# Linear attention and a squared-ReLU block on one core: values spread over the key features by broadcast DMAs instead of TensorE, normalised keys in a PSUM bank

## The reference, cut to what matters

```python
B, L, D, H, dk = 8, 512, 256, 16, 16
x = x + layernorm(attn(layernorm(x)))
x = x + layernorm(ffn(layernorm(x)))
# attn: q, k, v = x @ W_qkv.T, per head; k is normalised over its 16 features
def step(F, (q_t, k_t, v_t)):                 # scan over the 512 positions
    hebbian = einsum('bhd,bhe->bhde', v_t, k_t)
    F = retention * F + coef * hebbian        # retention, coef: [H, dk, dk]
    return F, einsum('bhde,bhe->bhd', W_LTM + F, q_t)
# y @ W_o.T follows
# ffn: y = square(relu(x @ W_fc.T)) @ W_proj.T, then a five-step spike count of y
```

## Time and profile before

| | before |
|---|---|
| median of 3 runs | 743.29 us (738.89 to 744.5) |
| profiled execution, own time | 738.58 us |
| its span | 736.8 us |
| TensorE busy | 605.3 us (82%) |
| VectorE busy | 544.8 us (74%) |
| GpSimd busy | 406.5 us (55%) |
| ScalarE busy | 338.1 us (46%) |
| DMA queue of SP | 20.02 MB, 7.8% of 16 engines |

### The profile page before, as it was taken

How to read it: one execution, slowest core, us unless ns; L and a number is a source line. 1 busy time by engine, 2 the same in 40 slices (tenths; PEclk the granted TensorE clock), 3 DMA queues, 4 the chain that set the end, 5 groups by cost and what they waited for, 6 DMA issues and landing times.

```text
span 736.8 us, 8225 instructions
## 1 busy us (share of the span) xinstructions
PE 605.3 (82%) x2760; PEld 407.2 (55%) x2768; DVE 544.8 (74%) x892; ACT 338.1 (46%) x631; POOL 406.5 (55%) x198
## 2 busy tenths in 40 slices
PE   0567778778999699988998899969998899778782
PEld 0343334435776477755775577647765576457471
DVE  4479999987898689977996789968996789722101
ACT  1422212333546644564446454664456433565644
POOL 0246775676468465865577546845586556631111
PEclk9969999899999999999999799999999999999897
DMA  7000100020000020002000110002000200020010
GB/s 262 28 0 1 57 1 0 1 85 1 0 1 30 0 87 1 29 1 87 0 30 1 50 37 1 28 2 85 1 1 1 86 1 0 1 85 1 0 58 28
DMA packets 16585, 21.58 MB, mean 29 GB/s; under 512 B 1184, under 2 KB 14880, under 8 KB 16416
## 3 DMA queue, kind: packets, MB, share of 16 engines
q1 hardware_dynamic: 16400, 20.02, 7.8%
q0 software_dynamic: 144, 1.05, 0.4%
HBM read 12.68 MB, written 4.19 MB: 23 GB/s over the span
## 4 chain that ended last, share of the span: by engine, by line
PE 54%; DVE 19%; issue 13%; ACT 8%; POOL 2%; DMA 2%; SPq 0%; POOLq 0%; ACTq 0%; DVEq 0%
PE p_c L358 10%; PE p_c L331 9%; DVE state L639 8%; PE p_a L253 8%; PE p_y L306 7%; PE p_rep L292 6%; DVE p_rep L630 5%; PE p_rep L293 5%; PE p_c L319 4%; ACT sign L510 3%; PE p_y L301 2%; DVE stats L595 2%; PE p_c L340 1%; POOL prod L757 1%; ACT x1f L445 1%
## 5 line engine op out<-in xcount | busy, mean ns | idle before, releaser
L757 POOL TENSOR_TENSOR prod<-state,qf 128x1024 f32<-128x1024 f32 x128 | 304.8, 2383 | 190.1 <-DVE state L639 188.0
L639 DVE TENSOR_TENSOR_SCAN state<-ret,p_rep 128x512 f32<-128x512 f32 x256 | 297.2, 1202 | 0.0
L630 DVE TENSOR_TENSOR p_rep<-p_rep,kf 128x1024 f32<-128x1024 f32 x128 | 156.4, 1222 | 75.4 <-PE p_rep L293 75.3
L292 PE MATMUL p_rep<-vh,pick_sb 128*128 128x512 f32 x256 | 118.2, 462 | 54.6 <-DVE state L639 48.3
L331 PE MATMUL p_c<-wproj_sb,ht 128*128 128x256 f32 x512 | 119.6, 383 | 1.3 <-ACT ht L500 1.3
L331 PEld LDWEIGHTS p_c<-wproj_sb,ht 128*128 128x128 f32 x512 | 95.1, 190 | 29.5 <-issue 15.1
L293 PE MATMUL p_rep<-vl,pick_sb 128*128 128x512 f32 x256 | 103.6, 405 | 0.0
L358 PE MATMUL p_c<-x1t,wfc_s 128*128 128x512 f32 x384 | 99.6, 404 | 3.3 <-ACT hr L498 3.3
L292 PEld LDWEIGHTS p_rep<-vh,pick_sb 128*128 128x128 f32 x256 | 50.0, 195 | 87.3 <-DVE state L639 70.0
L253 PE MATMUL p_a<-xt,wqkv_s 128*128 128x512 f32 x288 | 92.7, 464 | 4.6 <-issue 2.8
L358 PEld LDWEIGHTS p_c<-x1t,wfc_s 128*128 128x128 f32 x384 | 73.0, 194 | 23.2 <-issue 6.9
(11 more groups left out here) (92 smaller groups left out, 573.8 us busy)
## 6 DMA issues: line engine op xcount, KB each, us to landing
xa<-in_x SPq DMA_DIRECT2D x8, 512.0 KB, 3.5
x<-in_x SPq DMA_DIRECT2D x8, 512.0 KB, 3.4
x1k<-x SPq DMA_DIRECT2D x8, 512.0 KB, 2.9
out<-x1k SPq DMA_DIRECT2D x8, 512.0 KB, 2.8
pick_sb<-in_pick POOLq DMA_DIRECT2D x1, 1024.0 KB, 6.6
prod<-in_w_fc SPq DMA_DIRECT2D x1, 1024.0 KB, 8.0
wproj_sb<-in_w_proj SPq DMA_DIRECT2D x1, 1024.0 KB, 10.3
state<-in_w_qkv SPq DMA_DIRECT2D x1, 768.0 KB, 7.2
```

The lines of the kernel that those rows point to most:

```text
L292: pe.matmul(p_rep[s % 2][:, i, :], pick_sb[:, d, :], vh[:, half, :], start=True, stop=False)
L630: v.tensor_tensor(p_rep[s % 2][:, :, :], p_rep[s % 2][:, :, :], key, ALU.mult).then_inc(S["hebb_done"], 1)
L639: v.tensor_tensor_scan(state[:, s % NS, i, :], ret[:, r:r + 1].broadcast_to([P, L]), p_rep[s % 2][:, i, :], 0.0, ALU.mult, ALU.add).then_i ...
L757: p.tensor_tensor(prod[:, s % NZ, :, :], state[:, s % NS, :, :], qf[:, s // HS, :].unsqueeze(1).broadcast_to([P, 2, L]), ALU.mult).then_in ...
```

## The change

The four matmuls of a slot are gone, with `pick_sb`, `vh`, `vl`, the rounding on ScalarE and `low_v` on GpSimd. In their place, for each of the two features of a slot, the SP queue issues one DMA inside SBUF: the source is the 8 rows of `vf` that hold the feature (8 partitions x 512 values, 16 KB), each read 16 times, and the destination is one of 8 buffers `vrep` of 128x512 (256 KB). VectorE's product is cut into two instructions of 128x512; each reads `vrep` in SBUF and the normalised key `p_k`, which now lies in a PSUM bank, and writes one of three PSUM banks `p_u`. A buffer of `vrep` is filled again when the product 8 features earlier is done. The value projection now comes first of the three, so that the values are ready earlier, and turning the next input is a slot later. The key's normalisation of the second half moves from slot 6 to the start of slot 8, since there is one `p_k` for both halves. The copy `x1k` is gone: `x1` has two buffers in turn, and `store_out` and `load_again` stand between the broadcasts on the SP queue. The diff, cut (the same swap of order is made on ScalarE and in the prologue; semaphore names follow):

```diff
+NV = 8
+NU = 3
-        pick_sb = sb("pick_sb", [P, DK, P], F32R)
-        kf = sb("kf", [P, HALVES, L])
-        vf = sb("vf", [P, L])
-        vh = sb("vh", [P, HALVES, L], F32R)
-        vl = sb("vl", [P, HALVES, L], F32R)
+        vf = sb("vf", [P, HALVES, L])
+        vrep = sb("vrep", [P, NV, L])
-        x1 = sb("x1", [P, TILES, D])
-        x1k = sb("x1k", [P, TILES, D])
+        x1 = [sb(f"x1_{i}", [P, TILES, D]) for i in range(2)]
-        p_rep = [ps(f"p_rep{i}", [P, 2, L]) for i in range(2)]
+        p_u = [ps(f"p_u{i}", [P, L]) for i in range(NU)]
+        p_k = ps("p_k", [P, L])
...
+        v_in = [sem(f"v_in{i}") for i in range(NV)]
...
+            def spread_v(b, s):
+                half, features = step_features(s)
+                if s % HS == 0:
+                    sp.wait_ge(S["v_done"], 2 * b + half + 1)
+                for i, d in enumerate(features):
+                    n = 2 * (SLOTS * b + s) + i
+                    sp.wait_ge(S["hebb_done"], at(n - NV + 1))
+                    rows = vf[d * HH:(d + 1) * HH, half, :]
+                    sp.dma_start(vrep[:, n % NV, :], rows.unsqueeze(1).broadcast_to([HH, DK, L])).then_inc(
+                        v_in[n % NV], 16)
...
             load_x(1)
...
+            for g in range(B):
+                for s in range(SLOTS):
+                    spread_v(g, s)
+                    if s == 5 and g >= 3: store_out(g - 3)
+                    if s == 8 and g >= 1: load_again(g - 1)
+                    if s == 15 and g < B - 2: load_x(g + 2)
+            store_out(B - 3)
+            load_again(B - 1)
+            store_out(B - 2)
+            store_out(B - 1)
...
-            def replicate(b, s):
-                half, features = step_features(s)
-                if s % HS == 0:
-                    pe.wait_ge(S["v_low"], at(2 * b + half + 1))
-                for i, d in enumerate(features):
-                    pe.wait_ge(S["state_done"], at(2 * (SLOTS * b + s - 2) + i + 1))
-                    pe.matmul(p_rep[s % 2][:, i, :], pick_sb[:, d, :], vh[:, half, :], start=True, stop=False)
-                    last = pe.matmul(p_rep[s % 2][:, i, :], pick_sb[:, d, :], vl[:, half, :], start=False, stop=True)
-                last.then_inc(S["rep_done"], 1)
...
-                        if s == 0: project_k(g, 1)
-                        if s == 1: key_variance(g, 1)
-                        if s == 2: project_v(g, 1)
+                        if s == 0: project_v(g, 1)
+                        if s == 1: project_k(g, 1)
+                        if s == 2: key_variance(g, 1)
...
             def copy_v(b, half):
-                act.wait_ge(S["v_low"], at(2 * b + half))
-                copy(p_a[:, :], vf[:, :], "v_proj", 2 * b + half + 1, "v_done")
-                copy(vf[:, :], vh[:, half, :], "v_done", 2 * b + half + 1, "v_high")
+                act.wait_ge(S["hebb_done"], at(DK * (2 * (b - 1) + half + 1)))
+                copy(p_a[:, :], vf[:, half, :], "v_proj", 2 * b + half + 1, "v_done")
...
-                v.tensor_tensor(kf[:, half, :], p_a[:, :], kc[:, :], ALU.mult).then_inc(S["k_done"], 1)
...
+                dve.wait_ge(S["hebb_done"], DK * (2 * b + half))
+                v.tensor_tensor(p_k[:, :], p_a[:, :], kc[:, :], ALU.mult).then_inc(S["k_done"], 1)
+
+            def hebbian(b, s, i):
+                n = 2 * (SLOTS * b + s) + i
+                dve.wait_ge(v_in[n % NV], 16 * (n // NV + 1))
+                dve.wait_ge(S["state_done"], at(n - NU + 1))
+                if s % HS == 0 and i == 0:
                     dve.wait_ge(S["k_done"], at(2 * b + s // HS + 1))
-                key = kf[:, s // HS, :].unsqueeze(1).broadcast_to([P, 2, L])
-                v.tensor_tensor(p_rep[s % 2][:, :, :], p_rep[s % 2][:, :, :], key, ALU.mult).then_inc(
+                v.tensor_tensor(p_u[n % NU][:, :], vrep[:, n % NV, :], p_k[:, :], ALU.mult).then_inc(
                     S["hebb_done"], 1)
...
-                                     p_rep[s % 2][:, i, :], 0.0, ALU.mult, ALU.add).then_inc(S["state_done"], 1)
+                                     p_u[n % NU][:, :], 0.0, ALU.mult, ALU.add).then_inc(S["state_done"], 1)
...
+                    if now and s == HS: norm_k(g, 1)
...
-                    if now and s == 6: norm_k(g, 1)
...
-            def low_v(b, half):
-                rest(vf[:, :], vh[:, half, :], vl[:, half, :], "v_high", 2 * b + half + 1, "v_low")
-
-            p.dma_start(pick_sb[:, :, :], pick).then_inc(S["pick_in"], 16)
```

More of the change, by code:

```diff
@@ L210, in load_x @@
                 sp.dma_start(xa[:, :, :], by_tile(x, b)).then_inc(S["x_in"], 16)
[L212 to L223, removed]
@@ L225, in _ @@
-            load_x(1)
[L226 to L233, removed]
+            def spread_v(b, s):
[8 more added lines that the diff above has]
+                        v_in[n % NV], 16)
@@ new lines, in store_out, with load_again @@
+            def store_out(b):
+                sp.wait_ge(S["res_done"], at(b + 1))
+                sp.dma_start(by_tile(out, b), x1[b % 2][:, :, :]).then_inc(S["out_done"], 16)
+            def load_again(b):
+                sp.wait_ge(S["out_done"], at(16 * (b - 1)))
+                sp.dma_start(x1[b % 2][:, :, :], by_tile(x, b)).then_inc(S["again_in"], 16)
+            load_x(1)
+            for g in range(B):
[4 more added lines that the diff above has]
+                    if s == 15 and g < B - 2: load_x(g + 2)
@@ L416, in iteration @@
                             up(b1, 2)
-                    if after and s == SLOTS - 1: replicate(b, 0)
             run(iteration)
@@ L535, in iteration @@
                 for s in range(SLOTS):
-                    if now and s == 0: square_k(g, 1)
+                    if now and s == 0: copy_v(g, 1)
                     if two_before and s == 0: hidden(b2, 3)
                     if two_before and s == 1: hidden(b2, 4)
-                    if now and s == 1: key_deviation(g, 1)
+                    if now and s == 1: square_k(g, 1)
                     if two_before and s == 1: hidden(b2, 5)
-                    if now and s == 2: copy_v(g, 1)
+                    if now and s == 2: key_deviation(g, 1)
                     if before and s == 3: copy_y(b1, 1)
@@ L554, in iteration @@
                     if two_before and s == 13: signs(b2, 1)
-                    if after and s in (7, 8): copy_xt(b, s - 7)
+                    if after and s in (8, 9): copy_xt(b, s - 8)
                     if before and s == 10: deviation(3, b1)
-                    if after and s == 10: square_k(b, 0)
+                    if after and s == 10: copy_v(b, 0)
                     if now and s == 11: copy_y(g, 0)
-                    if after and s == 11: key_deviation(b, 0)
-                    if before and s == 11: norm(3, b1, x1, oo, "x1_done", b1 + 1)
+                    if after and s == 11: square_k(b, 0)
+                    if before and s == 11: norm(3, b1, x1[b1 % 2], oo, "x1_done", b1 + 1)
                     if before and s == 12:
@@ L563, in iteration @@
                         copy_x1t(b1, 1)
-                    if after and s == 12: copy_v(b, 0)
+                    if after and s == 12: key_deviation(b, 0)
                     if after and s == 13: copy_q(b, 0)
@@ L727, in iteration @@
                 for s in range(SLOTS):
-                    ends = (g, s - 1) if s > 0 else (b1, SLOTS - 1)
-                    if now: hebbian(g, s)
-                    if now if s > 0 else before: scan(*ends, 1)
-                    if now: scan(g, s, 0)
+                    if now and s == HS: norm_k(g, 1)
+                    first = s % HS == 0
+                    if now and not first: hebbian(g, s, 0)
+                    if s > 0 and now: scan(g, s - 1, 1)
+                    if s == 0 and before: scan(b1, SLOTS - 1, 1)
+                    if now:
+                        if first: hebbian(g, s, 0)
+                        hebbian(g, s, 1)
+                        scan(g, s, 0)
                     if after and s == 2: statistics(1, b, xa, "x_in", 16 * (b + 1))
@@ L735, in iteration @@
                     if before and s == 6: statistics(2, b1, oo, "o_done", 2 * (b1 + 1))
-                    if now and s == 6: norm_k(g, 1)
                     if before and s == 7: scales(2, b1)
-                    if before and s == 10: statistics(3, b1, x1, "x1_done", b1 + 1)
+                    if before and s == 10: statistics(3, b1, x1[b1 % 2], "x1_done", b1 + 1)
                     if before and s == 11: scales(3, b1)
@@ L796, in iteration @@
                     if s == 0 and before: read(b1, SLOTS - 1)
-                    if now and s == 4: low_v(g, 1)
                     if before and s == 8: add_attention(b1)
-                    if after and s in (8, 9): low_x(b, s - 8)
+                    if after and s in (9, 10): low_x(b, s - 9)
                     if before and s == 13:
@@ L802, in iteration @@
                         low_x1(b1, 1)
```

(1 more changed line is left out.)

51 lines of the change are left out of this document (21 added, 30 removed).

## The result

The changed kernel takes 1168.91 us (median of 4 runs, 1160.28 to 1171.25), the kernel before 742.1 in the same set. The ratio is 1.573, 95% interval 1.563 to 1.584: slower by 57%. The forecast was 1410 us with a range of 900 to 1600.

The account below looks back on a forecast made before the run. The prediction took the one DMA queue's broadcasts, bound by their few source partitions, to set the pace: 31.6 + 1262 + 23 + 0.6 + 94.8 = 1412 us of span, plus 1.8 outside it, 1414, rounded to 1410; range 900 to 1600.

Parts of the forecast that it names:

- The bound before, and what the change takes off: TensorE sets the pace at 81.3 us per iteration; losing 64 matmuls at 0.23 us takes off 14.7 us per iteration.
- The products: On VectorE, 32 products at 0.658 us replace 16 at 1224 ns: +1.5 us, 67.2 us busy per iteration.
- Start, whole-tile transfers, end: Outside the broadcasts: stream starts at 31.6 us, 18 whole-tile transfers take 23 us, last product to end takes 94.8 us.
- The broadcast, the deciding term: DMA queue: 256 broadcasts at 4.93 us each, 1262 us; an iteration cannot be shorter than 32 of them.
- c: Stream time of one 256 KB broadcast on the DMA queue; forecast 4.93 us, floor 0.62 to 1.23, ceiling 9.85.
- in between: Rival, chance 0.14: source gives more than twice a stream's rate, 2.3 to 4.4 us per broadcast; 997 us at 3.3.
- The likeliest case: Chance 0.66: DMA stream bound by its source, 4.4 to 5.7 us per broadcast, kernel 1280 to 1610 us.
- The doubling of a row's 26.6 GB/s: Broadcast source: twice the 26.6 GB/s of 8 partitions in the copy `x1k`, taken as 53.2 GB/s, 4.93 us per broadcast.
- The hidden rival: Rival, chance 0.17: broadcasts at most 1.23 us each are hidden, VectorE sets about 70 us per iteration, kernel 655 us.
- What the profile was to show: Signs: VectorE waiting for DMA over half the span, landing near eight times c, 67 MB more at some 50 GB/s.

## Why the prediction was right, and by how much

- **The bound before, and what the change takes off.** The 64 spreading matmuls of an iteration are gone. TensorE's pace no longer counts, as said: in the stretch from 300 to 500 us it is busy 109 of 200.
- **The products.** 0.658 us expected; 0.676 where they follow one another, 0.696 where VectorE had idled. VectorE's busy time in an iteration is 66.0 us with rows four apart, against 67.2.
- **Start, whole-tile transfers, end.** The first broadcast was issued at 29.9 (30.5 expected), and from the last product's start to the end it is 1168.1 - 1072.3 = 95.8 us (94.8).
- **The broadcast, the deciding term.** This is the step that was mis-sized: c = 4.93 us expected, 3.98 measured, 0.95 x 256 = 243 us, all of the difference between 1410 and 1169. The source's rate for one block, 53.2 GB/s as an estimate, was good: 51 measured with a fixed block. What failed is the sentence that blocks are read one after the other and that the eight buffers do not lift this. Overlap does lift it, where the next block is on another port: 2.97 us when every change of block allows it, 3.98 when every second does. By the Trainium skill (SBUF — State Buffer, Door 1: The DMA port swizzle) c would have been 4.82 us; for one block 5.10 was measured.
- **The case it fell in.** 3.98 us lies in the rival "in between" (2.3 to 4.4 us, chance 0.14), whose words were that streams share less evenly and blocks overlap; the overlap is what the runs show. The likeliest case (0.66) was 1280 to 1610 and did not come. The mechanism, a stream bound by its few source partitions, was right. The doubling of a row's 26.6 GB/s that priced one block had no row behind it; that it came out at 51 is luck as far as the rows go. The range held because it had been stretched down to 900.
- **The hidden rival.** Real once the rows are apart, and 712 to 717 us instead of 655, for the two reasons shown with that experiment: its price was 60 us too low.
- **What the profile was to show.** Right: VectorE waits for the DMA, the product at 0.7 us, no wait for TensorE. Nearly right: 63 MB more on the queue, not 67, because the copy `x1k` is gone. Too strong: VectorE idle before its product for over half of the span; it is 488 of 1168 us. Wrong: some 50 GB/s in every slice alike; it is 66 in the mean, at two rates. Wrong too: landing near eight times c, since eight are queued. A broadcast's product starts 13.4 us after SP took the broadcast up (median), 3.4 times c, and whole-tile transfers land after 10.6 to 11.3 us in place of 2.8 to 3.5. Its buffer lies free for 18.6 us before that, behind the held queue.

## What to carry to other kernels

Price a DMA by the narrower of its two ends: a broadcast from eight neighbouring partitions ran at those partitions' rate, 51 GB/s, while the queue had bytes waiting all the time, and one row read by more streams was slower still. Before giving it up, spread the source rows over the partitions: a layout of the weight's columns, free here, took a broadcast from 3.98 to 1.42 us in the mean and made a kernel 57% slower into one 4% faster. And when the term that decides is a rate no row shows, ask whether consecutive transfers share what limits them.

## What the runs showed of the hardware that I had not expected

- With no other block beside it, a source's rate went up in steps with the groups of four neighbouring partitions that it touches: 27 GB/s for one row, 51 for eight neighbours (two groups), 102 for rows two apart (four). Rows sixteen apart touch eight groups and gave 102 as well; rows four apart, also eight, gave 143 and later 205.
- A DMA queue that is held shows as issue time of its issuer: 3.99 us per broadcast in the changed kernel, 0.61 with spread rows, same instruction. An input load queued behind took 11.3 us to land, against 3.5 before.
- An SBUF operand moved to PSUM was worth 75 us (787 against 712), with the same instructions on VectorE and GpSimd.
- TensorE's granted clock fell with the waiting: 0.94 in the steady stretch before, 0.74 from 300 to 500 us after, 0.55 with one-row broadcasts. It cost little here: TensorE holds 3% of the changed kernel's chain.
